# Attention output units dealt out over six laps in place of four steps of every lap, and one landing report moved by one gather

## What is computed

```python
xn = _layernorm(x, axis=-1)
x = x + gnn(xn, src, dst, ...) + mix(xn[None], ...)[0]
x = x + ffn(_layernorm(x, axis=-1)[None], ...)[0]

# gnn, the edge part
e = leaky_relu(a_src . Wh[edge_row] + a_dst . Wh[edge_col]);  e = exp(e - max(e))
alpha = e / (segment_sum(e, edge_row)[edge_row] + 1e-15)
h_new = segment_sum(Wh[edge_col] * alpha, edge_row) + Wh

# mix, the two parts: over all rows of k and v first, then for every row of q
kv_mod = einsum('bhni,bhnj,bhne->bhije', kn, kn, vN);  kv = einsum('bhnd,bhne->bhde', kn, vN)
y = A * einsum('bhni,bhnj,bhije->bhne', qn, qn, kv_mod) + scale**2 * einsum('bhnd,bhde->bhne', qn, kv) + scale**4 * vsum
y = y[..., 1:] / y[..., :1];  out = y @ Wproj.T + bproj
```

## Time and profile before

| | us |
|---|---|
| median of 3 runs | 3717.87 (3713.49 to 3719.67) |
| the profiled execution | 3726.11 |
| its span | 3724.3 |
| key part, steps 0 to 207 (weighing starts 566.6 to 1609.3) | 1042.7 |
| output part, steps 208 to 403 (1609.3 to 2725.1) | 1115.8 |
| steps without unit, 404 to 435 (2725.1 to 2873.8) | 148.7 |
| last lap, steps 436 to 439, starts | 2873.8 to 2885.6 |

### The profile page before, as it was taken

How to read it: one execution, slowest core, us unless ns; L and a number is a source line. 1 busy time by engine, 2 the same in 40 slices (tenths; PEclk the granted TensorE clock), 3 DMA queues, 4 the chain that set the end, 5 groups by cost and what they waited for, 6 DMA issues and landing times.

```text
span 3724.3 us, 90309 instructions
## 1 busy us (share of the span) xinstructions
PE 2973.9 (80%) x23065; PEld 2188.1 (59%) x23065; DVE 2657.7 (71%) x6016; ACT 1913.5 (51%) x5687; POOL 2197.9 (59%) x2454
## 2 busy tenths in 40 slices
PE   4878737878877877889999999999976477777995
PEld 2334325545555555567777777777755266666894
DVE  9999997878878878877777777777765644535122
ACT  3777624434444444456666666666643134544663
POOL 4577647777767777776666666666667142244142
PEclk8787868989989989989999999999988768989997
DMA  2222225555555555554444444444444423344264
GB/s 64 87 92 90 80 70 149 139 143 141 136 144 142 141 142 140 141 138 123 120 121 125 120 120 120 120 123 120 121 115 114 146 88 114 105 142 134 93 182 121
DMA packets 324119, 453.01 MB, mean 122 GB/s; under 512 B 79008, under 2 KB 258398, under 8 KB 323736
## 3 DMA queue, kind: packets, MB, share of 16 engines
q0 software_dynamic: 86704, 239.52, 23.8%
q1 hardware_dynamic: 214428, 191.18, 18.5%
q10 hardware_dynamic: 22860, 20.83, 2.1%
HBM read 366.49 MB, written 84.82 MB: 121 GB/s over the span
## 4 chain that ended last, share of the span: by engine, by line
PE 31%; DVE 18%; issue 17%; POOL 14%; DMA 10%; ACT 5%; POOLq 3%; ACTq 2%; DVEq 1%; SPq 0%
POOL room L840 9%; DMA room<-table,room 8%; PE bank L2003 7%; PE bank L2037 5%; DVE room L1358 5%; PE bank L2199 4%; PE bank L2187 4%; DVE room L1357 4%; PE bank L2048 3%; POOL xs_dram L899 2%; POOLq L833 2%; PE bank L1991 2%; ACT room L1128 1%; PE bank L2069 1%; ACTq L1060 1%
## 5 line engine op out<-in xcount | busy, mean ns | idle before, releaser
L840 POOL DMA_INDIRECT room<-table,room x1564 | 1519.7, 972 | 727.3 <-issue 395.1
L2003 PE MATMUL bank<-room 128*128 128x260 f32 x3520 | 947.7, 416 | 255.7 <-DVE room L1543 154.3
L2003 PEld LDWEIGHTS bank<-room 128*128 128x128 f32 x3520 | 686.4, 205 | 382.1 <-issue 282.1
L1543 DVE TENSOR_TENSOR room<-room,bank 128x1024 f32<-128x1024 f32 x440 | 534.9, 1216 | 197.6 <-ACT bank L1073 191.9
L1560 DVE TENSOR_TENSOR room<-bank,room 128x1024 f32<-128x1024 f32 x392 | 477.2, 1217 | 0.0
L1066 ACT ACTIVATE spare<-away,ones 128x512 bf16<-128x512 bf16 x440 | 317.6, 722 | 53.1 <-ACT away L1063 2.3
L1063 ACT ACTIVATE away<-spare,minus_p 128x512 bf16<-128x512 bf16 x440 | 312.8, 711 | 2.1 <-DMA spare<-rows_dram 1.9
L1515 DVE TENSOR_TENSOR room<-iota_f,row_step 128x512 f32<-128x512 f32 x440 | 301.3, 685 | 0.3 <-DVE row_step L1449 0.3
L1073 ACT ACTIVATE bank<-room 128x16 f32<-128x16 f32 x440 | 81.4, 185 | 428.4 <-DVE room L1537 414.4
L1842 DVE TENSOR_TENSOR planes<-bank,spare 128x256 f32<-128x256 f32 x119 | 50.5, 425 | 332.6 <-PE bank L2199 306.1
L2199 PE MATMUL bank<-room 128*128 x952 | 238.1, 394 | 51.2 <-DVE planes L1842 51.0
(11 more groups left out here) (314 smaller groups left out, 4831.8 us busy)
## 6 DMA issues: line engine op xcount, KB each, us to landing
spare<-rows_dram SPq DMA_DIRECT2D x440, 128.0 KB
room<-table,room POOLq DMA_INDIRECT x1564
kv_dram<-room SPq DMA_DIRECT2D x49, 324.0 KB, 2.2
room<-kv_dram SPq DMA_DIRECT2D x196, 81.0 KB
y_dram<-planes SPq DMA_DIRECT2D x119, 128.0 KB, 1.7
room<-xs_dram ACTq DMA_DIRECT2D x110, 128.0 KB, 2.2
q_dram<-room SPq DMA_DIRECT2D x49, 192.0 KB, 1.8
room<-q_dram SPq DMA_DIRECT2D x196, 48.0 KB
```

The lines of the kernel that those rows point to most:

```text
L840: pool.indirect_dma_start(G[:, k.slot, u, :], None, table, bass.IndirectOffsetOnAxis(ap=ixbuf[:, k.slot, u:u + 1].bitcast(I32), axis=0)).t ...
L1543: dve.tensor_tensor(Gw[:, h, :, 0:C].rearrange("p u (h d) -> p u h d", h=GH), G[:, bass.ds(slot, 1), :, 0:C].rearrange("p a u (h d) -> p ( ...
L2003: ins = pe.matmul(pbank[1 + h][:, 0:TW], OH[:, s, u, :], Gw[:, h, u, :], start=(u == 0), stop=(u == U - 1))
```

## The change

The 49 x 4 output units are dealt out differently. The first nine tiles (`HEAD`) keep one unit per step (laps 52 to 60). The other 40 tiles take the 48 laps 61 to 108 in 8 rounds of six laps and five tiles: of 24 steps in a round 20 have a unit, and every sixth step has none (`unit_at`). So there is no separate stretch without units, except for the last lap. The closing of the last tile now stands in front of that last lap. PE, DVE, ACT and SP use the same table; their loops over rounds have a body of six laps in place of one (ACT runs seven rounds in its loop and writes the eighth out). Within a step the order of the pieces stays.

The second edit: POOL's `report` of group k-1 moves from behind the second gather of group k to behind the third.

```diff
+    HEAD = 9
+    ROUND_LAPS, ROUND_TILES = 6, 5
+    Q_ROUNDS = (NT - HEAD) // ROUND_TILES
+    def unit_at(i, r, s):
+        n = 4 * r + s
+        if n % ROUND_LAPS == ROUND_LAPS - 1:
+            return None
+        v = n - n // ROUND_LAPS
+        return i * ROUND_TILES + (HEAD + v // 4), v % 4
+    def round_lap(i, r):
+        return i * ROUND_LAPS + (LAPS_K + HEAD + r)
...
-                if u == 1 and k.after(1):
+                if u == 2 and k.after(1):
                     report(k + -1)
...
+        def q_middle(at):
+            def middle(s):
+                if at(s) is not None:
+                    ft_part(*at(s))
+            return middle
+
+        def q_lap(i, at):
+            lap(i, q_extra(at), q_middle(at))
...
-        with pe.Fori(1, NT) as q:
-            lap(q + LAPS_K, q_extra(q), lambda s: ft_part(q, s))
+        with pe.Fori(1, HEAD) as q:
+            q_lap(q + LAPS_K, lambda s: (q, s))
+        with pe.Fori(0, Q_ROUNDS) as i:
+            for r in range(ROUND_LAPS):
+                q_lap(round_lap(i, r), lambda s: unit_at(i, r, s))
         tail_part(NT - 1, 0)
         tail_part(NT - 1, 1)
         tail_part(NT - 1, 2)
-        with pe.Fori(LAPS_K + NT, LAPS - 1) as i:
-            lap(i)
         lap(LAPS - 1)
```

More of the change, by code:

```diff
@@ L611, in _ @@
                 load_row(At(LAPS_K + q + 1, s, 4))
-        with sp.Fori(2, NT) as q:
+        with sp.Fori(2, HEAD) as q:
             for s in range(4):
@@ L616, in _ @@
             store_mix(q - 2)
+        with sp.Fori(0, Q_ROUNDS) as i:
+            for r in range(ROUND_LAPS):
+                for s in range(4):
+                    load_row(At(round_lap(i, r + 1), s, 4))
+                    if unit_at(i, r, s) is not None:
+                        q, u = unit_at(i, r, s)
+                        load_q(q, u)
+                        if u == 3:
+                            store_mix(q - 2)
         store_mix(NT - 2)
         store_mix(NT - 1)
-        with sp.Fori(LAPS_K + NT + 1, LAPS) as i:
-            for s in range(4):
-                load_row(At(i, s, 4))
         sp.wait_ge(s_edges_end, 1)
@@ L1100, in next_k, with next_q, lap @@
             return copy
[L1102 to L1108, removed]
+        def next_q(q, s):
+            if s < 3 or not isinstance(q, int) or q < NT - 1:
+                copy_q(q + (s + 1) // 4, (s + 1) % 4)
+        def lap(i, unit=None, at=None):
             for s in range(4):
                 k = At(i, s, 4)
+                q, u = (at(s) if at is not None else None) or (None, None)
                 if (k + 3).inside(STEPS):
@@ L1114, in lap @@
                     unit(s)
-                if mode == "q" and s == 0 and not (isinstance(q, int) and q == 0):
-                    copy_yst(q - 1)
+                if q is not None:
+                    next_q(q, u)
+                    if u == 0 and not (isinstance(q, int) and q == 0):
+                        copy_yst(q - 1)
                 if (k + 1).inside(STEPS):
                     exps(k + 1)
-                if mode == "q":
-                    q_part(q, s)
+                if q is not None:
+                    q_part(q, u)
         def copy_yt():
@@ L1177, in _ @@
             act.sem_inc(kvt_copied, 1)
-        lap(LAPS_K, "q", 0, next_q(0))
+        lap(LAPS_K, at=lambda s: (0, s))
         base = o.count
-        with act.Fori(1, NT - 1) as q:
+        with act.Fori(1, HEAD) as q:
             o.laps(q - 1, base, PER + 2)
-            lap(q + LAPS_K, "q", q, next_q(q))
-        o.count = base + (PER + 2) * (NT - 2)
-        lap(LAPS_K + NT - 1, "q", NT - 1, next_q(NT - 1))
+            lap(q + LAPS_K, at=lambda s: (q, s))
+        o.count = base + (PER + 2) * (HEAD - 1)
+        base = o.count
+        per = ROUND_LAPS * PER + ROUND_TILES * 2
+        with act.Fori(0, Q_ROUNDS - 1) as i:
+            o.laps(i, base, per)
+            for r in range(ROUND_LAPS):
+                lap(round_lap(i, r), at=lambda s: unit_at(i, r, s))
+        o.count = base + per * (Q_ROUNDS - 1)
+        for r in range(ROUND_LAPS):
+            lap(round_lap(Q_ROUNDS - 1, r), at=lambda s: unit_at(Q_ROUNDS - 1, r, s))
         copy_yst(NT - 1)
@@ L1188, in _ @@
         copy_mix(NT - 1)
-        base = o.count
-        with act.Fori(LAPS_K + NT, LAPS - 1) as i:
-            o.laps(i - (LAPS_K + NT), base, PER)
-            lap(i)
-        o.count = base + PER * (LAPS - 1 - LAPS_K - NT)
         lap(LAPS - 1)
@@ L1607, in lap, with q_extra @@
             dve.reg_mov(slot_reg, slot)
-        def q_extra(q):
+        def q_extra(at):
             def extra(s):
-                q_features(q, s)
-                if s == 1 and not (isinstance(q, int) and q == 0):
-                    normalise_y(q - 1)
+                if at(s) is not None:
+                    q, u = at(s)
+                    q_features(q, u)
+                    if u == 1 and not (isinstance(q, int) and q == 0):
+                        normalise_y(q - 1)
             return extra
@@ L1643, in _ @@
                 dve.sem_inc(kvc_copied, 1)
-        lap(LAPS_K, q_extra(0))
+        lap(LAPS_K, q_extra(lambda s: (0, s)))
         base = o.count
         per = 4 * STEP + 2
-        with dve.Fori(1, NT) as q:
+        with dve.Fori(1, HEAD) as q:
             o.laps(q - 1, base, per)
-            lap(q + LAPS_K, q_extra(q))
-        o.count = base + per * (NT - 1)
-        normalise_y(NT - 1)
[L1652 to L1657, removed]
+            lap(q + LAPS_K, q_extra(lambda s: (q, s)))
+        o.count = base + per * (HEAD - 1)
+        base = o.count
+        per = ROUND_LAPS * 4 * STEP + ROUND_TILES * 2
+        with dve.Fori(0, Q_ROUNDS) as i:
+            o.laps(i, base, per)
+            for r in range(ROUND_LAPS):
+                lap(round_lap(i, r), q_extra(lambda s: unit_at(i, r, s)))
+        o.count = base + per * Q_ROUNDS
+        normalise_y(NT - 1)
         lap(LAPS - 1)
@@ L2101, in _ @@
         pe.wait_ge(s_w3, 16)
-        lap(LAPS_K, q_extra(0), lambda s: ft_part(0, s))
-        with pe.Fori(1, NT) as q:
-            lap(q + LAPS_K, q_extra(q), lambda s: ft_part(q, s))
+        q_lap(LAPS_K, lambda s: (0, s))
+        with pe.Fori(1, HEAD) as q:
+            q_lap(q + LAPS_K, lambda s: (q, s))
+        with pe.Fori(0, Q_ROUNDS) as i:
+            for r in range(ROUND_LAPS):
+                q_lap(round_lap(i, r), lambda s: unit_at(i, r, s))
         tail_part(NT - 1, 0)
```

14 lines of the change are left out of this document (8 added, 6 removed).

## The result

The changed kernel takes 3666.4 us (median of 4 runs, 3660.7 to 3668.5) against 3718.8 for the kernel before: a ratio of 0.9868, 95% interval 0.9855 to 0.9882, or 52 us less. The forecast was 101 us less. The direction held; half of the gain did not come.

What follows compares the result with a forecast made beforehand. POOL was taken to bound the key part and the steps without unit, PE the output part; -57 - 59 - 4 + 19 = -101 us from the profiled 3726.1 gives 3625, 3617 after 8.2 us to the median; range 3580 to 3685.

Steps and rivals of the forecast that it cites:

- The bounds of the three stretches: Whole edge part: POOL sets the pace in the key part, PE in the output part, POOL in 32 steps without unit.
- The report: Key part: awaiting the landing one gather later fills 1.25 us of each of 82 waits; -57 us, bounds -69 and -15.
- Rival (1): Key part: transfers hold the gathers, POOL's waits just move to the fourth gather; gain 15 instead of 57, 3659 us; chance 0.12.
- The spreading: Output part: 32 steps without unit, moved among steps with one, cost 89.6 instead of 148.7 us; -59, bounds -72 and -16.
- The price of a bare step: Output part: a step without unit costs 2.8 us, the middle between PE's 2.39 and DVE's 3.08 and 3.14.
- Rival (2): Output part: scores, exponentials, weighing restart after each step without unit, costing 4.15 us; gain 16 instead of 59, 3660 us; chance 0.12.
- The sign that I named for it: Output part: starts of weighings 2.4 to 3.1 us apart around each step without unit; 4 or more would support the rival.
- The longer loop bodies: Round loops: code drawn anew each round stalls PE 2.7 us at each of seven jumps back, DVE's and ACT's covered; +19 us.
- The upper bound that I gave for this term: Round loops: jump stalls of PE, DVE and ACT one after another; 57 us.
- The small terms: End of kernel: ACT's 1.91 us for a row falls, last lap's starts 9.3 instead of 11.8 us apart; together -4 us.
- What would have shown it: Output part: instruction packets from about 1900 us on, some 80 on PE's queue, and a PE gap at each of seven jumps.
- Rival (6): Whole kernel: stalls of all three engines (57 us) meet both weak gains, nothing net; about 3717 us; chance 0.03.

Runs made afterwards that it cites:

- report_only_b: The kernel before with only POOL's report moved behind the third gather, units left as they were: 3664.8 us, ratio 0.9874.
- pe_straight: The changed kernel with its eight rounds written out on PE alone, DVE and ACT still jumping back: 3627.7 us, ratio 0.9774 against the kernel before.

## Why the prediction missed

**The bounds of the three stretches** were read rightly: POOL, PE, POOL.

**The report, -57 forecast, -49 measured.** The mechanism held. The landing wait fell by 74.4 us in the view of waits, and 8.5 of them came back as the ordinary gaps (189.2 us for issue in place of 180.7), which leaves 66, more than forecast. What took part of it back is a term that I didn't have: the gathers became longer. The 740 of the key part, before and after:

```profile
566.60:1609.30 1042.70, 723.36 (x740) 0.91 0.56 141
```

```profile
565.80:1559.60 993.80, 741.90 (x740) 0.94 0.59 148
```

That is 18.5 us, and 66 - 18.5 is the 49, but for 2 us. By the medians the report is worth 46 us alone (`report_only_b`) and 39 to 41 on top of the written-out rounds. Why the gathers become longer when they follow more closely is not shown. DVE's wait for the report shrank from 149.1 to 104.7 us though each report may come later, as forecast. Rival (1), that the wait just moves, fell.

**The spreading, -59 forecast, -70 measured without the jumps** (1065.3 to 994.9 us). The price of a bare step, 2.8 us, was nearly right: 2.6 us where nothing else is in the way, 124.4 us per round against 125 forecast. Rival (2), which gave a bare step 4.15 us, would be nearer to the changed kernel's 4.7 by its number, and is wrong as a mechanism: the same order of work without jumps has 2.6. The sign that I named for it, starts of weighings 2.4 to 3.1 us apart around each bare step, is poor: of the four bare steps of a written-out round two show it (3.1 and 3.0 us), the others have 4.9 and 5.9.

**The longer loop bodies, +19 forecast, +66 measured** (994.9 to 1061.4 us). This is the step that failed, and it failed in its size. I had the mechanism, the count (seven jumps) and the sign from the Trainium skill (Runtime: NRT & Kernel Launch, Instruction fetch mechanics) and from the earlier trace rows, and three things wrong behind them:
- I took 2.7 us for one packet's trip (the two terms named for it, 1.7 and 1.25, even make 2.95; either is too small). The branch takes 3.8 to 4.85 us.
- I counted one stop per jump. There are two on PE, since the second packet isn't there either (1.2 to 2.85 us after the first transposes), and some 10 us at half the clock with them.
- I took DVE's and ACT's jumps as covered because they fall in a bare step, ahead of PE. They cost 25 to 31 us: PE is the bound, but it waits for the features that DVE makes behind its jump, 2.5 to 3.0 us at each of the seven places in `pe_straight`.

The upper bound that I gave for this term, 57 us, assumed all three engines one after another and was still too low. With what was measured, -49 - 70 + 66 = -53 us for the key part and the rounds; the -8 us of the other rows of the table make the 60.6 between the two profiled executions, and the medians lie 52 apart.

**The small terms.** The last lap came at 10.4 us (forecast 9.3). The closing of the last tile costs no more in its new place: the weighings on either side of it lie 8.5 us apart, 12.4 before.

**What would have shown it** did: 148 - 55 = 93 more packets on PE's queue (forecast some 80), and the seven gaps. The range, 3580 to 3685, held the time, in part by luck: the fetch term lay above its own bound, and the spreading, 11 us better than forecast, made up for some of it. Rival (6) had its sum wrong: stalls of 57 us against weak gains of 15 + 16 + 4 make 3740, not 3717.

## What to carry to other kernels

Before a loop body is unrolled several times over, count its instructions on every engine, not just on the busiest, and compare with bodies that the profile shows to stay loaded (no packets on the instruction queues inside the loop); if it is larger, write the loop out or keep it small, since what costs here is the jump back (66 us for seven jumps on three engines), not the straight code. A wait for a landing inside a queue that sets the pace belongs behind the next work of that queue: here one gather later gave 1.3%, and a second one nothing that could be told.

## What the runs showed of the hardware

- A jump back in a loop body that is drawn anew held PE for 3.8 to 4.85 us and then for 1.2 to 2.85 us again, with one packet on its instruction queue in each stop, and the granted clock was 0.50 from 2157 to 2167 us at the third jump. ACT stood idle 2.65 and 2.98 us ahead of its first operation behind the jump in the two places shown.
- PE kept 4.5 packets of 256 instructions (1158) and not 6.4 (1627). DVE and ACT kept 1.7 and 1.3 packets of 128 and not 2.7 and 2.2.
- Straight code drew 132 packets on PE's queue with no such stop, at PE 936 of 995 us busy.
- With the waits for landings down from 93.8 to 19.4 us, the 740 indirect gathers of the key part went from 723.4 to 741.9 us; over the program a gather went from 0.972 to 0.990 us.
- On two occasions the kernel before took 4715 and 4819 us in place of some 3715, on the first of them on the chip that has number 9 in both states; PE paused there 0.5 to 1.2 us between independent matmuls (in the lines shown). Neither edit gained.
